# Moving the copy of K out of PSUM from VectorE to ScalarE, and reordering VectorE's statistics and the first loads, in an 8-core macaron block

## The reference

```
x  = x + 0.5 * LN(x) @ sign(Wf).T                     # FFN1, gives y1
Q, K, V = LN(x) @ Wq.T + bq, @ Wk.T + bk, @ Wv.T + bv # 16 heads of 64
Q, K = phi(Q), phi(K)
KV = K^T V;  Z = sum of K over the rows               # for each sequence and head
x  = x + (Q KV / (Q . Z + 1e-6)) @ Wo.T + bo          # gives y2
x  = x + 0.5 * LN(x) @ sign(Wf).T                     # FFN2, the output
```

## Time and profile before

| | |
|---|---|
| time, median of 6 runs | 2016.03 us (2013.65 to 2156.47) |
| the profiled execution's own time | 2017.81 us |
| its span on core 6 | 2016.1 us |
| spans of the 8 cores | 2009.9 to 2016.1 us |
| busy in the span: PE | 1769.6 us (88%) |
| busy in the span: ACT | 1171.6 us (58%) |
| busy in the span: DVE | 842.4 us (42%) |
| busy in the span: POOL | 147.5 us (7%) |
| granted PE clock, mean | 0.990 |

### The profile page before, as it was taken

One profiled execution on the slowest core, in us unless ns is written; L12 is line 12 of the kernel. 1 busy time (PEld: TensorE's weight loads), 2 busy tenths in 40 slices (PEclk: granted clock), 3 DMA queues, 4 the chain that ended last, 5 costly groups with the idle time before them and its releaser, 6 DMA issues.

```text
span 2016.1 us, 33065 instructions; the slowest of 8 cores (2009.9 to 2016.1 us)
## 1 busy us (share of the span) xinstructions
PE 1769.6 (88%) x10784; PEld 793.8 (39%) x10784; DVE 842.4 (42%) x2177; ACT 1171.6 (58%) x1897; POOL 147.5 (7%) x274
## 2 busy tenths in 40 slices
PE   0499999999999999999999999788888888888887
PEld 0143444444344344444434443344444444444443
DVE  2144444444444444444444443234444444444443
ACT  1377667767766766776776676444444444444443
POOL 1000000000000010000000000001010101010100
PEclk9899999999999999999999999899999999999999
DMA  8722222222222233222222221233333333333332
GB/s 174 138 67 92 94 69 93 92 77 85 92 94 69 92 102 104 80 93 93 70 92 92 89 74 61 67 116 120 116 120 116 111 125 112 125 116 121 117 119 79
DMA packets 134630, 199.34 MB, mean 99 GB/s; under 512 B 88384, under 2 KB 88384, under 8 KB 134464
## 3 DMA queue, kind: packets, MB, share of 16 engines
q0 software_dynamic: 32960, 109.08, 16.3%
q1 hardware_dynamic: 101504, 88.15, 14.4%
HBM read 104.87 MB, written 83.89 MB: 94 GB/s over the span
## 4 chain that ended last, share of the span: by engine, by line
PE 69%; ACT 13%; DVE 8%; issue 6%; DMA 3%; DVEq 1%; ACTq 0%; SPq 0%
PE pA L465 35%; PE pA L476 23%; DVE y2t L346 4%; PE pA L480 4%; ACT u1b L444 4%; PE pA L470 3%; ACT u2b L450 3%; DVE kbK L312 2%; ACT kbQ L390 2%; DMA y3t<-wfT 2%; DMA stg<-wfT 2%; PE tpB L455 2%; ACT nb L362 1%; PE pKa L523 1%; ACT r L361 1%
## 5 line engine op out<-in xcount | busy, mean ns | idle before, releaser
L465 PE MATMUL pA<-sw,u2fm 128*128 128x512 bf16 x1024 | 236.2, 384 | 76.9 <-DVE y2t L346 75.7
L476 PE MATMUL pA<-wv,u1fm 128*128 128x512 bf16 x1024 | 242.4, 379 | 25.6 <-DVE kbK L312 25.6
L476 PE MATMUL pA<-wk,u1fm 128*128 128x512 bf16 x1024 | 242.3, 379 | 18.6 <-ACT kbQ L390 18.6
L444 ACT ACTIVATE u1b<-y2t 128x1024 bf16<-128x1024 f32 x64 | 67.6, 1056 | 301.5 <-DVE y2t L346 301.5
L465 PE MATMUL pA<-wo,attnfm 128*128 128x512 bf16 x1024 | 234.8, 383 | 5.4 <-DVE y3t L326 1.1
L465 PE MATMUL pA<-sw,u0fm 128*128 128x512 bf16 x1024 | 237.0, 385 | 0.0
L465 PE MATMUL pA<-wq,u1fm 128*128 128x512 bf16 x1024 | 232.1, 380 | 0.0
L465 PEld LDWEIGHTS pA<-sw,u2fm 128*128 128x128 bf16 x1024 | 96.9, 99 | 196.1 <-issue 93.3
L346 DVE SCALAR_TENSOR_TENSOR y2t<-pA,y1in 128x1024 f32<-128x1024 f32 x64 | 78.4, 1225 | 188.4 <-PE pA L470 188.4
L312 DVE CAST kbK<-pA 128x512 bf16<-128x512 f32 x64 | 44.3, 692 | 252.8 <-PE pA L480 252.8
L476 PEld LDWEIGHTS pA<-wv,u1fm 128*128 128x128 bf16 x1024 | 90.3, 97 | 140.4 <-issue 49.5
(11 more groups left out here) (120 smaller groups left out, 2432.3 us busy)
## 6 DMA issues: line engine op xcount, KB each, us to landing
xt<-x SPq DMA_DIRECT2D x64, 512.0 KB, 3.7
y1scr<-y1t POOLq DMA_DIRECT2D x64, 512.0 KB, 3.8
y1in<-y1scr POOLq DMA_DIRECT2D x64, 512.0 KB, 4.0
out<-y3t SPq DMA_DIRECT2D x64, 512.0 KB, 2.6
qscr<-qfm POOLq DMA_DIRECT2D x64, 256.0 KB, 3.1
qfin<-qscr POOLq DMA_DIRECT2D x64, 256.0 KB, 4.1
qfm<-phiQ SPq DMA_TRANSPOSE x512, 2.3
stg<-wfT SPq DMA_DIRECT2D x4, 512.0 KB, 8.9
```

The lines of the kernel that those rows point to most:

```text
L444: e.activation(u1b[:, 0, :], y2t[:, tw % 2, :], AF.Square, accum_out=sq3b[:, :]).then_inc(sSq3, 1)
L465: mm = e.matmul(dst[:, h*512:(h+1)*512], lhs_fm[:, c*P:(c+1)*P], w_sb[:, c, h*512:(h+1)*512], start=(c == 0), stop=(last and c == 7))
L476: mm = e.matmul(dst[:, h*512:(h+1)*512], lhs_fm[:, c*P:(c+1)*P], w_sb[:, c, h*512:(h+1)*512], start=(c == 0), stop=(last and c == 7))
```

## The change

Three edits. On SP, the first two chunks of `wfT` are issued ahead of the first four x tiles; the body of the chunk loop becomes a function that is called for chunks 0 and 1, then the x tiles are loaded, then come chunks 2 to 7 with the same waits. On DVE, the statistics of LN2 get a set of small operations of their own, directly behind y1, ahead of the sum and the squares of LN1, and those of LN1 get a second set behind these. And the two copies of K go from DVE's list to ACT's, behind the three operations on Q.

```
         @block.sync
-            for t0 in range(4):
-                e.dma_start(out=xt[:, t0 % 4, :], in_=x[...]).then_inc(dIn[t0 % 4], 16)
-            for c in range(8):
+            def stg_chunk(c):
                 buf = stg[:, 0, :] if c % 2 == 0 else y3t[:, 0, :]
                 if c >= 2:
                     e.wait_ge(sSw, c - 1)
                 if c >= 1:
                     e.wait_ge(gStg, 16 * c)
                 e.dma_start(out=buf, in_=wfT[c*P:(c+1)*P, :]).then_inc(gStg, 16)
+            stg_chunk(0)
+            stg_chunk(1)
+            for t0 in range(4):
+                e.dma_start(out=xt[:, t0 % 4, :], in_=x[...]).then_inc(dIn[t0 % 4], 16)
+            for c in range(2, 8):
+                stg_chunk(c)
...
         @block.vector, first pass, behind y1
+                if t + 1 < NT:
+                    v.wait_ge(sSq2, t + 2)
+                    if t >= 2:
+                        v.wait_ge(sR02, t)
+                    ln_stats_multi(v, vsync, [(red2b, sq2b, vr2, (t + 1) % 2, negm2, mS2)]
+                                   )[0].then_inc(vVr2, 1)
                 if t + 3 < NT:
                     tf = t + 3
                     v.wait_ge(dIn[tf % 4], 16 * (tf // 4 + 1))
                     v.reduce_sum(red1b[:, :], xt[:, tf % 4, :], axis=AX.X)
                     vsync(v, v.scalar_tensor_tensor(y2t[:, 0, :], xt[:, tf % 4, :], ...,
                                            ALU.bypass, ALU.mult, accum_out=sq1b[:, :]))
-                specs = []
...
-                    outs = ln_stats_multi(v, vsync, specs)
...
                     if t >= 1:
                         v.wait_ge(sR01, t)
+                    ln_stats_multi(v, vsync, [(red1b, sq1b, vr1, (t + 3) % 4, negm1, mS1)]
+                                   )[0].then_inc(vVr1, 1)
...
-                v.wait_ge(tK, t + 1)
-                v.tensor_copy(kbK[:, 0:512], pA2[:, 0:512]).then_inc(vKbK, 1)
-                v.tensor_copy(kbK[:, 512:1024], pA2[:, 512:1024]).then_inc(vKbK, 1)
...
         @block.scalar, first pass, behind mxb of Q
+                e.wait_ge(tK, t + 1)
+                e.copy(kbK[:, 0:512], pA2[:, 0:512]).then_inc(vKbK, 1)
+                e.copy(kbK[:, 512:1024], pA2[:, 512:1024]).then_inc(vKbK, 1)
                 e.wait_ge(vKbK, 2 * t + 2)
                 e.wait_ge(vPhiQ, t + 1)
```

More of the change, by code:

```diff
@@ L158, in _ @@
         def _(e):
-            for t0 in range(4):
-                s, j = t0 // NJ, t0 % NJ
-                e.dma_start(out=xt[:, t0 % 4, :], in_=x[s, j*P:(j+1)*P, :]).then_inc(dIn[t0 % 4], 16)
-            for c in range(8):
+            def stg_chunk(c):
                 buf = stg[:, 0, :] if c % 2 == 0 else y3t[:, 0, :]
@@ L168, in _ @@
                 e.dma_start(out=buf, in_=wfT[c*P:(c+1)*P, :]).then_inc(gStg, 16)
+            stg_chunk(0)
+            stg_chunk(1)
+            for t0 in range(4):
+                s, j = t0 // NJ, t0 % NJ
+                e.dma_start(out=xt[:, t0 % 4, :], in_=x[s, j*P:(j+1)*P, :]).then_inc(dIn[t0 % 4], 16)
+            for c in range(2, 8):
+                stg_chunk(c)
             for t in range(NT):
@@ L290, in _ @@
                                            ALU.bypass, ALU.mult, accum_out=sq1b[:, :]))
-                specs = []
[L292 to L297, removed]
                     if t >= 1:
                         v.wait_ge(sR01, t)
-                    specs.append((red1b, sq1b, vr1, (t + 3) % 4, negm1, mS1))
-                if specs:
-                    outs = ln_stats_multi(v, vsync, specs)
[L303 to L306, removed]
+                    ln_stats_multi(v, vsync, [(red1b, sq1b, vr1, (t + 3) % 4, negm1, mS1)]
+                                   )[0].then_inc(vVr1, 1)
                 if t + 2 < NT:
```

## The result

The changed kernel takes 2126.96 us in the median of its runs, against 2015.45 us of the kernel before: a ratio of 1.0536, with a 95% interval of 1.0515 to 1.0556. That is slower, as forecast, but by 111 us where I had said 72, and outside the range of 2076 to 2102. Times given as a range leave out the executions in which all cores of a die ran at a lower clock; ratios leave out those that this made clearly longer, so that the ratios of two experiments, the copy ahead of mxb and the start without the weight loads, still hold one or two of them and stand a little high.

The account below looks back on a forecast made before the run. The first pass was taken as a PE loop with almost no air, where any longer PE wait is paid in full. 2017.8 + 72 - 1 = 2089, or 2087 from the median, gave 2088 us, range 2076 to 2102.

Parts of the forecast that it names:

- The late copy: First pass: ACT's copy of K behind mxb starts V 1.14 us later in 63 tiles, +72 us, bounds +56 to +89.
- The swap of the statistics: First pass, DVE: LN2's statistics ahead of LN1's gain nothing and u0fm stays covered, costed at 0.
- The start: Loads before the first projection: two weight chunks ahead of the x tiles, -1 us, bounds -9 to +17.
- the lower bound: Start: if POOL's weight loads start 2.5 us later, chunk 3 slips through at 3.6 us, -9 us.
- The clock falls: Rival, first pass: V runs at 1.2 GHz behind PE's longer wait, 151 us more, some 2240 us; 4 in 100.
- The price per fallen tile: In the clock rival: V's 16 matmuls cost 6.03 in place of 3.63 us, 2.4 us a tile.

Follow-up runs that it names:

- the copy ahead of mxb: Changed kernel with ACT's copies of K put before mxb of Q: 2066.6 and 2067.5 us, ratio 1.0285.
- the start without the weight loads: Kernel before with the new order of loads and POOL's weight loads held until seven chunks have landed: 1996.8 to 2002.6 us, ratio 0.9947.
- The run with 1.59 us: Kernel before, K still copied on DVE but behind two unused copies of 512 columns each: 2132.2 to 2133.7 us, ratio 1.0583.
- the late copy on DVE: Kernel before, K still copied on DVE behind two unused copies, at 1.52 us of wait 512 and 448 columns wide: 2081.1 and 2082.4 us.

## Why the prediction was right and wrong

*The late copy: right.* It was costed at 1.14 us in 63 tiles; the period went from 18.50 to 19.62 or 19.63. On core 6 the stretch from the first to the last copy of Q grew from 1166.3 to 1235.9 us, by 69.6, where 72 was forecast. Wait, engine, length and total (97.3 us for some 95) came as said; mnb waits no more for phiQ. With the start this makes 2016 + 70 - 8 = 2078 us, and the slowest core that kept its clock took 2079.

*The swap of the statistics: right.* It measures 0. In the timeline lnb still starts 0.15 us behind the second copy of Q, and u0fm has 8.3 us of cover (512.91 to 521.21).

*The start: the lower bound came true.* The term was -1 and measured -8. The step that was off is where the weight loads meet the chunks: I had them at 19.63 as before. They leave 1 to 2 us later and chunk 3 is issued 1 to 2 us earlier, so it slips through at 3.7 us, and that is the bound of -9 with the mechanism given for it. The bias loads do move with SP's order: bkr's issue waits 3.84 us for bqr, with only chunk 1 and the first x tiles issued, and bvr's waits 7.14 us for bkr, beside the x tiles and chunk 2.

*The rival "The clock falls": the step that failed.* The sum priced PE's longer wait at its length alone and had no term for the clock; some 50 us on the slowest core is what was missing. I gave the fall 4 in 100, as a case in which V runs at the lower clock in all tiles or none, on all cores, and judged it by the second pass, which waits 1.18 us at a clock of 1.00. That row shows only that 1.18 us is on the safe side. It doesn't say how far the border is, and PE's 1.52 us stood on it: at 1.51 us the tiles kept their clock, at 1.52 to 1.53 three cores lost it in part of their tiles and others did not, at 1.59 every core lost it in every second or third tile.

The trace of the kernel before had more to say than that row. Here is FFN2 of the second pass, on core 6, behind those of its waits for y2t that are longer than 1.3 us:

```profile
1338.56 5.30 PE L465 MATMUL pA<-sw,u2fm 128*128 128x512 bf16 x16 [1.34 <-DVE y2t L346]
1519.21 5.30 PE L465 MATMUL pA<-sw,u2fm 128*128 128x512 bf16 x16 [1.53 <-DVE y2t L346]
1978.81 3.61 PE L465 MATMUL pA<-sw,u2fm 128*128 128x512 bf16 x16 [1.53 <-DVE y2t L346]
2001.23 5.19 PE L465 MATMUL pA<-sw,u2fm 128*128 128x512 bf16 x16 [1.84 <-DVE y2t L346]
```

Behind three of the four it takes 5.2 to 5.3 in place of 3.61 us, and behind a wait of 1.53 us, the very length that I forecast for V, once so and once not. From 1518 to 1526 us the granted clock is 0.79; the mean of 1.00 over 600 us hides it. So that a wait of this length can cost the clock, and not each time, stood in the trace that I read, and 4 in 100 was far too little.

The price per fallen tile was over-sized (1.6 us against 2.4, as only V's first half is slowed), and the choice of all or nothing was wrong: the case between, one or two cores with every second tile, costs about 31 x 1.6 = 50 us, and the metric takes just that core.

The Trainium skill, TensorE: Matmul & The Clock Gate, section on HAM oscillation, tells of a kernel in which a wait in every tile makes PE throttle again each time. The run with 1.59 us shows this in kind, in every second tile; that a wait as short as that does it is from the rows here.

## What to carry to other kernels

A wait that repeats in every tile has two prices: its length, and the matmuls behind it if PE's clock falls; look at every core's span and granted clock, because one core with a fallen clock is the whole metric. When a change makes PE's wait longer, look in the trace of before at the matmuls behind PE's few longest waits, one by one, since a mean clock hides them; if any of them is slowed, price a case in which a part of the tiles and cores falls. A copy moved to an engine with a low busy share costs what that engine does at that moment, not what the share says.

## What the runs showed of the hardware

- Standing still for 1.59 us in a tile of 19.7 us was enough for a granted clock of half in the matmuls behind it, in every second tile of all cores. Behind 1.51 us no tile fell; at 1.52 to 1.53 us three cores fell, and with the late copy on DVE none. The border is that of this loop: in the second pass of the kernel before, matmuls behind a wait of 1.34 us were slowed.
- With one unused matmul of 128 columns in the wait, 1.46 us were left of it and no core fell; with six, 0.23 us, also none, on the chip on which cores fell without them.
- With the same wait of 1.59 us, a tile of 19.91 in place of 19.69 us had every third tile fall in place of every second.
- Cores that run the same program differ by 0.01 to 0.02 us in the same wait, and with the late copy on ACT the three cores with the longer one were the three that lost their clock.
- A chunk of the weight took 3.6 us when it was issued 1.1 us ahead of the first of POOL's weight loads, 11.6 us when it was issued 1.7 us behind it, and later chunks 8.6 to 10.2 us beside them; that one chunk is the 7 to 8 us that the new start gains.
